# Attention with expert routing on one core: the residual add taken earlier, the experts' lists kept whole, and the hand-over prepared ahead

## The reference, cut to what matters

```python
x = x + xattn(layernorm(x), ctx, Wq, Wk, Wv, Wo, q_norm_w, k_norm_w)   # 64 x 128 x 512
n = layernorm(x).reshape(8192, 512)
rw, sel = top_k(softmax(n @ gate_w.T), 2)          # 12 experts; rw divided by its sum
# expert e: the first 854 entries of [all first choices, then all second choices] that chose e
h = silu(n[tok] @ w1[e].T * (n[tok] @ w3[e].T)) @ w2[e].T          # F = 64
out = out.at[tok].add(h * w[:, None])
```

## Time and profile before

| | before |
|---|---|
| median of 3 runs | 2482.19 us (2481.06 to 2484.36) |
| the profiled execution's own time | 2481.01 us |
| its span, first to last instruction | 2479.1 us |
| busy share of the span | PE 92%, DVE 75%, ACT 71%, POOL 45% |
| mean granted TensorE clock | 0.961 of full speed |

### The profile page before, as it was taken

How to read it: one execution, slowest core, us unless ns; L and a number is a source line. 1 busy time by engine, 2 the same in 40 slices (tenths; PEclk the granted TensorE clock), 3 DMA queues, 4 the chain that set the end, 5 groups by cost and what they waited for, 6 DMA issues and landing times. The chain is left out here.

```text
span 2479.1 us, 54081 instructions
## 1 busy us (share of the span) xinstructions
PE 2271.0 (92%) x12931; PEld 1152.0 (46%) x12931; DVE 1869.0 (75%) x5158; ACT 1766.7 (71%) x6911; POOL 1125.1 (45%) x1949
## 2 busy tenths in 40 slices
PE   3899999999999999999999999999999999468884
PEld 1344444444444444444444444445444444244442
DVE  6778888888888888888888888888888887436554
ACT  5877777777777777777777777777777777234442
POOL 4334444444444444444444444444444443268875
PEclk9899999999999999999999999999999999778886
DMA  8477766666777667676676777667676766359997
GB/s 256 94 140 138 140 139 138 136 134 137 136 144 141 137 137 144 138 137 137 137 136 135 135 142 143 136 135 141 140 139 137 136 135 119 83 144 188 182 177 93
DMA packets 894363, 348.08 MB, mean 140 GB/s; under 512 B 829004, under 2 KB 829260, under 8 KB 894288
## 3 DMA queue, kind: packets, MB, share of 16 engines
q1 hardware_dynamic: 867520, 297.06, 60.3%
q0 software_dynamic: 22912, 43.16, 9.8%
q10 hardware_dynamic: 3888, 7.38, 0.8%
HBM read 91.37 MB, written 57.71 MB: 60 GB/s over the span
## 5 line engine op out<-in xcount | busy, mean ns | idle before, releaser
L824 PE MATMUL pb<-wo,o 128*128 128x512 f16 x3072 | 709.8, 381 | 61.6 <-DVE work L1164 50.3
L954 ACT ACTIVATE work<-pb,small 128x128 f32<-128x128 f32 x1024 | 455.2, 453 | 165.1 <-DVE small L1139 165.1
L1407 POOL TENSOR_TENSOR small<-small 128x4 f32<-128x4 f32 (+1 forms) x584 | 485.4, 835 | 54.0 <-POOL small L1478 13.8
L824 PEld LDWEIGHTS pb<-wo,o 128*128 128x128 f16 x3072 | 287.1, 98 | 397.5 <-issue 61.2
L1478 POOL TENSOR_TENSOR small<-small 128x4 f32<-128x4 f32 x256 | 84.2, 329 | 697.3 <-ACT junk_q L935 691.6
L755 PE MATMUL pb<-wq,xT 128*128 128x512 f16 x1536 | 356.4, 382 | 0.9 <-DVE q L1127 0.9
L755 PE MATMUL pb<-wq,wkv_raw 128*128 128x512 f16 x1536 | 352.4, 379 | 0.6 <-DVE q L1127 0.6
L1127 DVE SCALAR_TENSOR_TENSOR q<-pb,small,q 128x128 f16<-128x128 f32 x1024 | 288.3, 344 | 71.7 <-ACT q L944 71.7
L968 ACT ACTIVATE o<-pb 128x512 f16<-128x512 f32 x256 | 153.1, 598 | 222.4 <-PE pb L812 221.8
L944 ACT ACTIVATE q<-pb,small 128x128 f16<-128x128 f32 x1024 | 291.1, 365 | 4.6 <-DMA qT<-q 4.5
L935 ACT ACTIVATE junk_q<-pb 128x128 bf16<-128x128 f32 x1024 | 273.4, 305 | 6.4 <-PE pb L755 6.4
(11 more groups left out here) (152 smaller groups left out, 3546.1 us busy)
## 6 DMA issues: line engine op xcount, KB each, us to landing
work<-x SPq DMA_DIRECT2D x128, 256.0 KB, 3.0
work<-c SPq DMA_DIRECT2D x64, 256.0 KB, 4.0
out<-work SPq DMA_DIRECT2D x64, 256.0 KB, 2.1
xn_scratch<-work SPq DMA_DIRECT2D x64, 256.0 KB, 2.3
wo_raw<-wo ACTq DMA_DIRECT2D x4, 1024.0 KB, 9.1
qT<-q SPq DMA_TRANSPOSE x256
pT<-p SPq DMA_TRANSPOSE x256
wq_raw<-wq ACTq DMA_DIRECT2D x3, 1024.0 KB, 11.3
```

The source lines that it names most:

```text
L824: mm = nc.tensor.matmul(WO_B[:, :], o16[:, HPG * a + h, :], part(O0 + g, b_)[:, h, :], start=(g == 0 and h == 0 and n == 0), stop=(g == NG ...
L954: ex = nc.scalar.activation(probs[:, cols], S_B[:, cols], ACT.Exp, bias=nmax[:, h:h + 1], scale=esc, accum_out=psums[:, h:h + 1])
L1407: return nc.gpsimd.tensor_tensor(out_, in_, neghalf[:, 0:n], ALU.pow)
```

## The change

- `residual(b - 1)` moves, on DVE in slot 2, from behind `normalise` to ahead of `norm_k`.
- An expert's list is one stretch of 896 rows: first choices from row 0 upwards, second choices from row 853 downwards. For this `choose` makes a third mask, PE counts all first choices for the second's expert (four small matmuls for two), and `place` has one operation more. A scatter waits for the one before to land. No `join`, no totals.
- SP loads all lists at the end of the attention with three DMAs (expert 0, expert 1, experts 2 to 11) into one tile that gather and add both read. `from_i`, `to_i`, `load_from` and `load_to` are gone.
- The first two experts' weights are loaded in slot 2 of block 2, the gather tiles are cleared in the attention's last slots, both in the room of the raw attention weights, which are not read any more by then.
- The experts' loops are written out.

```diff
@@ DVE, the attention's slot @@
+                        if g == 2 and live(b - 1):
+                            residual(b - 1)
                         if g == 2 and live(b + 1):
                             norm_k(b + 1)
...
-                        if g == 2 and live(b - 1):
-                            residual(b - 1)
                         if live(b):
                             split_p(*cur)
@@ PE, positions @@
-                    nc.tensor.matmul(R_B[:, POS_C], tri[:, :], mask, start=True, stop=False)
-                    nc.tensor.matmul(R_B[:, POS_C], ones_b[:, :], macc[:, :],
-                                     start=False, stop=True).then_inc(pos_done, 1)
+                    own, every = R_B[:, POS_C][:, 0:2 * E], R_B[:, POS_C][:, 2 * E:3 * E]
+                    nc.tensor.matmul(own, tri[:, :], mask[:, 0:2 * E], start=True, stop=False)
+                    nc.tensor.matmul(own, ones_b[:, :], macc[:, :], start=False, stop=True)
+                    nc.tensor.matmul(every, ones_b[:, :], mask[:, 0:E], start=True, stop=False)
+                    nc.tensor.matmul(every, ones_b[:, :], macc[:, 0:E], start=False, stop=True).then_inc(pos_done, 1)
@@ DVE, choose and place @@
+                    nc.vector.tensor_copy(idxf[:, 2:3], idx8[:, 1:2])
...
+                    nc.vector.tensor_tensor(pos3[:, 2:3], pos3[:, 2:3], pos3[:, 1:2], ALU.add).then_inc(pl_step, 1)
...
+                    nc.vector.tensor_tensor(pos_s, pos3[:, 0:2], list_sign, ALU.mult).then_inc(pl_step, 1)
...
-                    nc.vector.scalar_tensor_tensor(out=over[:, 0:1], in0=idxf[:, 0:1], scalar=float(STRIDE),
-                                                   in1=over[:, 0:1], op0=ALU.mult, op1=ALU.add)
-                    nc.vector.scalar_tensor_tensor(out=over[:, 1:2], in0=idxf[:, 1:2], scalar=float(CP),
-                                                   in1=over[:, 1:2], op0=ALU.mult, op1=ALU.add).then_inc(pl_step, 1)
+                    nc.vector.scalar_tensor_tensor(out=over, in0=idxf[:, 0:2], scalar=float(CP), in1=over,
+                                                   op0=ALU.mult, op1=ALU.add).then_inc(pl_step, 1)
@@ SP @@
+                def first_expert_weights():
+
+                    sp.wait_ge(w_lo, NC * len(SPLIT))
+                    for i in range(2):
+                        sp.dma_start(w13_s[i], w13[i]).then_inc(d_w13[i], 16)
+                        for half in (slice(0, F), slice(F, 2 * F)):
+                            sp.dma_start(w2_s[i][half, :], w2T[i]).then_inc(d_w2[i], 16)
...
+                        if g == 2 and isinstance(b, int) and b == 2:
+                            first_expert_weights()
 
                 loop(sp, body)
+                sp.wait_ge(d_sent, 32)
+                sp.wait_ge(lists_set, 1)
+                sp.wait_ge(s_table, 32 * NB)
+                for i, (lo, hi) in enumerate(((0, 1), (1, 2), (2, E))):
+                    load_lists(i, lo, hi)
@@ POOL @@
-                    wait_apart(pool, (dst_rdy, b + 1), (w1_done, b + 1))
+                    wait_apart(pool, (dst_rdy, b + 1), (w1_done, b + 1), (s_table, 32 * b))
...
+                        if isinstance(b, int) and (b, g) in ((NB - 1, 3), (NB, 1)):
+                            nc.gpsimd.memset(xg[0 if b < NB else 1], 0.0).then_inc(s_z, 1)
@@ experts, on each engine @@
-            with pool.Fori(1, PAIRS - 2) as j:
+            for j in range(1, PAIRS - 2):
```

More of the change, by code:

```diff
@@ L20 @@
 CP = NT * 128
[L23 to L25 removed]
+ROWS = E * CP
 BIG = 1 << 20
@@ L168, in _ @@
+            for e in range(2, E):
+                j, i = e // 2, e % 2
+                wait_apart(sp, (h_done, 2 * (e - 1)))
+                sp.dma_start(w13_s[i], w13[e]).then_inc(d_w13[i], 16)
+                wait_apart(sp, (w2_lo_done, e - 1))
+                for half in (slice(0, F), slice(F, 2 * F)):
+                    sp.dma_start(w2_s[i][half, :], w2T[e]).then_inc(d_w2[i], 16)
         @block.gpsimd
@@ L187, in scatter_add @@
                     nc.gpsimd.indirect_dma_start(
-                        out=out, out_offset=bass.IndirectOffsetOnAxis(ap=to_i[i][:, t, 0:1], axis=0),
+                        out=out, out_offset=bass.IndirectOffsetOnAxis(ap=lists[:, e, t, 0:1], axis=0),
                         in_=yb[i][:, t, :], in_offset=None, compute_op=ALU.add).then_inc(d_add[i], 16)
-            for tile in from_i + to_i:
-                nc.gpsimd.memset(tile[:, :, 1], 0)
-                nc.gpsimd.iota(tile[:, :, 0], pattern=[[1, NT]], base=T, channel_multiplier=NT).then_inc(s_z, 1)
-            for i in range(2):
-                nc.gpsimd.memset(xg[i][:, :, :], 0.0).then_inc(s_z, 1)
-            pool.wait_ge(s_z, 6)
+            pool.wait_ge(s_z, 2)
             for e in range(3):
@@ L263, in step @@
                 down(j, i)
-            nc.tensor.matmul(pb[0][:, 0:2 * E], ones_b[:, :], macc[:, :], start=True, stop=True).then_inc(s_tot, 1)
             transposes(0, 0)
@@ L270, in _ @@
             step(0, 1)
-            with pe.Fori(1, PAIRS - 1) as j:
+            for j in range(1, PAIRS - 1):
                 step(j, 0)
@@ L333, in step @@
                     split_w2(j + i, 1 - i)
-            act.wait_ge(s_n, 1)
-            for e in range(1, E, 2):
-                join(act, e)
             first_half(0, 0, more=False)
@@ L342, in _ @@
             step(0, 1)
-            with act.Fori(1, PAIRS - 1) as j:
+            for j in range(1, PAIRS - 1):
                 step(j, 0)
@@ L393, in _ @@
             step(0, 1)
-            with dve.Fori(1, PAIRS - 1) as j:
+            for j in range(1, PAIRS - 1):
                 step(j, 0)
@@ L1244, in place @@
+                    nc.vector.tensor_tensor(over, over, pos_s, ALU.add).then_inc(pl_step, 1)
+                    wait(dve, pl_step, base + 10)
                     nc.vector.tensor_tensor(dst, over, list_off, ALU.add).then_inc(dst_rdy, 1)
```

185 lines of the change are left out of this document (62 added, 123 removed).

## The result

| | before | after |
|---|---|---|
| median | 2481.62 us (4 runs, 2480.93 to 2484.36) | 2417.43 us (4 runs, 2413.91 to 2418.82) |
| the profiled execution's own time | 2481.01 us | 2416.92 us |
| its span | 2479.1 us | 2415.2 us |
| ratio of the times | | 0.9737, 95% interval 0.972 to 0.9754 |

The account below looks back on a forecast made before the run. PE was taken to bound the attention and POOL the experts. 50.2 + 2.3 - 0.6 + 8.4 + 2.4 - 1.5 - 0.3 = 60.9 us off the profiled 2481.0 gave 2420.1, median 2421 us; range 2409 to 2438.

Parts of the forecast that it names:

- residual in the loop: Attention loop: PE's wait for the residual goes, its slot falls from 8.71 to 7.90 us; 50.2 us saved over 62 blocks.
- last block: End of the attention: the residual can stand right behind split_o, so everything after out_project comes 2.3 us earlier.
- longer routing behind it: Last two blocks: the longer choose and place lie in the chain twice and cost 0.6 us.
- clears: Attention's last slots: clearing xg on POOL may hold DVE operations through the shared port; 0.3 us lost, 0 to 3.1 allowed.
- weights in block 2: SP's queue in block 2: six weight DMAs delay the turns of q and k; 1.5 us lost (0 to 4).
- hand-over: Last scatter to first gather: clears moved, joins gone, list asked for earlier; first gather at 2163.1, not 2171.54, 8.4 us saved.
- up to expert 3: First gather to the gather of expert 3: the list is already at hand, 2.4 us saved.
- from there to the end: Gather of expert 3 to the end: POOL bounds, same indirect DMAs, so its 267.6 us stay as they are.
- Rival 1: Attention: DVE becomes the bound and the attention gives 25 us less, 2446 us; chance 0.13.
- rival 2: First experts run better than before, as PE's some 8 us late signal of expert 0 goes: 2413 us; chance 0.14.
- Rivals 3 and 4: 3: early residual holds DVE, 2485 us and more, chance 0.03; 4: big list or straight code delays first gathers, 2433, 0.07.

Follow-up runs that it names:

- the residual alone: Kernel before with one edit, residual(b - 1) moved ahead of norm_k on DVE: 2421.42 us, ratio 0.9763.
- the third gather held back: Changed kernel with POOL issuing the gathers of expert 2 only when PE's up of expert 0 is done: 2412.88 us, ratio 0.9763.
- the two kernels with added operations: Changed kernel with two or five useless DVE operations more in each block of the loop: 2410.02 us (ratio 0.9752) and 2460.24 us (0.9948).
- the first set: Four follow-up kernels run together on one chip: residual moved alone, residual put back, clears left out, weights loaded in the drain; the kernel before took 2480.8 us there.
- the weights in the drain: Changed kernel with the first experts' six weight DMAs issued in slot 1 of block 65, not slot 2 of block 2: 2418.7 us, ratio 0.975.
- the second and third set: Later follow-up runs, four kernels each, on another chip; the kernel before took 2471.4 and 2473.1 us, the changed kernel 2410.68 us in the third.

## Why the prediction held, step by step

The median was forecast within 4 us. Term by term it was less exact, and part of the closeness is luck: the clears were 2.3 us worse than counted and the first experts 2.8 better. The measured terms come to 63.7 us, the spans differ by 63.9, and 60.9 were predicted. Two things that the table leaves out nearly cancel: in the changed kernel's profile PE's first scores come 1.5 us later (57.8 for 56.4), and the blocks up to the last give 1.8 more than the 62 of the loop term.

| term | predicted | measured | from |
|---|---|---|---|
| residual in the loop | 50.2 | 51.2 | (32.323 - 31.497) x 62 |
| last block | 2.3 | 1.2; 3.5 with the old routing | the last block's slots 1 and 2: 18.47 before, 17.24 after, 14.94 with the residual alone |
| longer routing behind it | -0.6 | -0.4 | last scores to last scatter: 28.4 with the old routing (residual alone), 28.8 with the new and no clears |
| clears | -0.3 | -2.6; -1.0 to -1.75 without PE's clock | last scatter with and without them |
| weights in block 2 | -1.5 | -1.15 | slot 3 of block 2: 8.94 for 7.79 |
| hand-over | 8.4 | 8.9 | 13.8 and 4.9 |
| up to expert 3 | 2.4 | 5.2 | 39.94 and 34.75 |
| from there to the end | 0 | 1.3 | within the 2.4 by which this stage varies |

**The residual.** The mechanism and the size were right, shown from both sides: moved alone it gives 2.37% of the time before, taken back it costs 2.32%. The slot of 7.90 was met by 7.89. What I had not seen is that the same move is worth more without the other edits: the two further small matmuls cost 0.050 us in each block (31.497 against 31.447), 3.1 us in all.

**The last block** was right in its mechanism, and the size as well: PE's wait for the residual there fell from 4.25 to 1.95 us, 2.3 less, as predicted. The stage shows 1.2 because two things take from it. The longer `choose` and `place` cost 0.6 in these slots (15.54 with the third gather held back, 14.94 with the residual alone, both with the second series of `out_project` at full clock) and 0.4 behind them, 1.0 where 0.6 was counted. The rest is PE's clock: the second series took 4.43 us in the changed kernel, 4.03 in the kernel before and 2.75 with the residual alone.

**DVE's room** was mis-sized. I counted about 0.25 us left in a block; the two kernels with added operations show 0.83. Part of the error is in the price of the longer routing (0.3 to 0.4 counted, 0.1 measured), the rest in the reading: I took the idle time ahead of `maxima` as all there was, but the changed kernel shows 0.55 a block of it, and slots without such idle time give way by 0.2 us too. Rival 1 had less behind it than its 0.13.

**The clears** were priced too low. I had argued that most of DVE's work there reads two inputs or PSUM. That is true, but one operation that does not, `norm2`, stands in the chain, and holding it cost 1.0 us; where the second clear's `CAST` began early it cost 0.75 more. The remaining 1.7 of the 2.6 is one series of `out_project` at half clock, which five kernels with the same clears did not have; why it falls on this series in one run and not in another stays open. The rule of the Trainium skill (SBUF: State Buffer, two separate sides) fits what was held and what was not: held were a `TENSOR_SCALAR` with one SBUF input (1.70 us for 0.54) and a `CAST` of two elements (0.97 and 2.65 for 0.16), not held the `TENSOR_TENSOR` of 128 x 512 with two inputs (0.69 as ever), which by the same section has to wait for GpSimd only if that reads SBUF, and a memset does not.

**The hand-over** went as drawn: 3.9 us from the end of the last scatter's issue (2110.24) to the first gather, where 4.4 were expected. The list of ten experts was never waited for. The DMA view shows when it was in: SP's queue moved 1470 packets between 2111 and 2118.4 and none from there to 2135, while the gather of expert 2 started at 2132.51.

```profile
q1 hardware_dynamic: 1470, 0.08, 13.6%
```

The three loads have 12 x 122 = 1464 rows, so six packets are left, two a load. That fits the Trainium skill's rule (DMA: Bandwidth & Descriptors, Why a DMA increments its semaphore by 16 and not by 1) by which 122 partitions give two engines; no view shows the engines one by one.

**The first experts** gained more than the list, 5.2 us for 2.4, and rival 2 may have a part in it. In the first set and in the result's pair the second half of `up` of expert 0 reached ACT 16.8 us after its start in the kernel before and in the one with the residual alone, 11.0 in the changed kernel and with the residual put back, and 11.1 with the weights in the drain; the rows of the matmuls end 8.1 to 8.6 us after the start in all five. So this lateness is no property of the attention, and it was shorter with the new hand-over. But the kernel without the clears, of the same set, had only 8.7, and its way to expert 3 was 34.2 us all the same. There ACT waited 2.4 and 2.2 us ahead of its copies of expert 1, which it doesn't in the third set:

```profile
2133.47 0.48 ACT L217 COPY h<-pb 64x384 f32<-64x384 f32 x1 [2.59 <-PE pb L143]
...
2138.46 0.58 ACT L210 COPY xgT<-pb 128x512 f32<-128x512 f32 x1 [2.44 <-remote]
```

So the second half is one of several late signals. In the second and third set there are none: the changed kernel takes 27.9 us for this stage, at nearly the same clock and with the same instructions and gathers in flight. That rules out clock and code as sole causes. These two sets ran on another chip than the first, and whether that is the cause was not tested; it stays open.

Rivals 3 and 4 did not occur: DVE waited for the residual's x 0.9 us once, and neither the list nor straight code held anything.

## What to carry to other kernels

Look at the slot, not at the shares: one operation that stands two places too late on an engine with room cost 2.4%, and the rest of a large change 0.3%. Work that is moved out of a hand-over into the main part is not free because an engine is idle there; each piece was paid somewhere, in an issue queue (1.15 us), in operations held beside a memset (1.0 to 1.75), in the bounding engine's own small instructions (3.1), and spreading or dropping the pieces afterwards gave back 6.4. To learn how much room an engine has, add useless work until the time moves; its idle time ahead of one instruction told two thirds of it (0.55 of 0.83), and the prediction from the kernel before a third. And before a stage's 2 or 3 us are put down to an edit, look for a kernel with the same instructions there: here such a pair was 3.7 us apart.

## What the runs showed of the hardware

- A memset on GpSimd (3.1 us) holds some DVE operations until it ends and not others: `TENSOR_SCALAR` 128 x 512 in fp32 took 1.70 us instead of 0.54; a `CAST` of 128 x 2 took 0.97 instead of 0.16, and 2.65 where it began earlier in the memset; a `CAST` of 128 x 1 and a `TENSOR_TENSOR` 128 x 512 were unchanged.
- An indirect scatter of 128 rows of 8 bytes can land late: DVE waited 3.34 us for it with 1 MB of loads issued in the same 3 us, 1.31 and 2.66 us in two kernels without such loads, and not at all in the others. The cause is not shown.
- In the changed kernel's last block, where PE waits 1.2 to 3.1 us ahead of each `out_project`, its granted clock falls to half for a part of the time (the mean from 2072 to 2076 us is 0.62), and a series of twelve matmuls then took 4.4 us instead of 2.76. Which of the series it is differs between kernels with the same instructions there, and moves the last scatter by up to 1.7 us each.
- A signal of PE can reach other engines up to 8 us after the rows of its matmuls end, in the first profiles and in the first set of runs, and in none of the eight profiles taken on another chip.
